# Local attention with stationary values in four column groups and weights normalised ahead of the transpose; causal mask added on VectorE; new instruction orders

## What is computed

```python
# block 1: attention, 16 heads of 64;  block 2: routed spline network (cheap, long chain of small steps)
# block 3, L1_attn
lin = linear_attention(h @ wq_lin, h @ wk_lin, h @ wv_lin)
# 16 heads of 8 channels, each query sees the keys at distance -32..32
s = q_loc . k_loc / sqrt(8) + rel_bias[offset, head];  a = softmax(s over the 65 offsets);  win = a @ v_loc
gate = sigmoid(relu([lin, win, h] @ wg1 + bg1) @ wg2 + bg2)
x = gate * lin + (1 - gate) * win, then @ wo + bo
# block 4, L1_ffn: sequences of 256, handled as the sub-sequences that the reference's shapes give
attn = softmax(causal(10 * l2norm(q) @ l2norm(k)));  16 heads of 64
moe = sum_e gate_e * (gelu(h @ w1_e + b1_e) @ w2_e + b2_e), 8 experts of 512
```

## Time and profile before

| | |
|---|---|
| runs | 2386.63, 2387.47, 2390.48 us (median 2387.47) |
| profiled execution, span from first to last instruction | 2377.5 us |
| PE (TensorE) busy | 2234.4 us, 94% |
| DVE (VectorE) busy | 1557.1 us, 65% |
| ACT (ScalarE) busy | 1348.7 us, 57% |
| POOL (GpSimd) busy | 847.3 us, 36% |
| chain that ended last | PE 77%, DVE 12%, ACT 5%, POOL 4% |
| mean granted TensorE clock | 0.986 |

### The profile page before, as it was taken

One profiled execution on the slowest core, in us unless ns is written; L12 is line 12 of the kernel. 1 busy time (PEld: TensorE's weight loads), 2 busy tenths in 40 slices (PEclk: granted clock), 3 DMA queues, 4 the chain that ended last, 5 costly groups with the idle time before them and its releaser, 6 DMA issues.

```text
span 2377.5 us, 44469 instructions
## 1 busy us (share of the span) xinstructions
PE 2234.4 (94%) x16347; PEld 1546.4 (65%) x16347; DVE 1557.1 (65%) x4247; ACT 1348.7 (57%) x3784; POOL 847.3 (36%) x1010
## 2 busy tenths in 40 slices
PE   8999999999999999999999999999999999999897
PEld 5565666856667566676667666676666756667465
DVE  5677676676657766577765867558675676656752
ACT  5346464764547755476545757466564764646452
POOL 3315551064510643116521356114561054510630
PEclk9999999999999999999999999999999999999999
DMA  4000001000010000110001000001001000010001
GB/s 149 28 1 1 1 2 45 10 32 1 1 54 11 23 1 1 54 33 1 1 10 45 32 1 1 27 28 32 1 1 45 10 32 1 1 36 10 32 1 49
DMA packets 24722, 50.46 MB, mean 21 GB/s; under 512 B 3316, under 2 KB 3900, under 8 KB 24252
## 3 DMA queue, kind: packets, MB, share of 16 engines
q1 hardware_dynamic: 24508, 47.63, 6.2%
HBM read 45.52 MB, written 2.10 MB: 20 GB/s over the span
## 4 chain that ended last, share of the span: by engine, by line
PE 77%; DVE 12%; ACT 5%; POOL 4%; issue 2%; DMA 0%; SPq 0%; DVEq 0%; ACTq 0%
PE ps L1494 10%; PE ps L1515 10%; PE ps L651 5%; PE ps L668 5%; PE ps L602 5%; PE ps L868 4%; PE ps L1428 4%; PE ps L906 4%; PE ps L1527 4%; PE ps L1445 4%; PE ps L799 3%; PE ps L782 3%; PE ps L835 2%; PE ps L1383 2%; PE ps L1394 2%; POOL rn L1737 2%
## 5 line engine op out<-in xcount | busy, mean ns | idle before, releaser
L1048 POOL TENSOR_TENSOR rstd<-ve,half_neg 128x4 f32<-128x4 f32 (+1 forms) x56 | 66.8, 1193 | 971.9 <-DVE ve L1029 971.9
L1515 PEld LDWEIGHTS ps<-wbuf,QK 128*128 128x128 f32 x2048 | 266.0, 191 | 108.2 <-issue 99.9
L1304 POOL TENSOR_TENSOR E<-E,ri 128x512 f32<-128x512 f32 x240 | 247.4, 1039 | 180.4 <-DVE ri L1103 180.2
L1618 ACT ACTIVATE QK<-ps,cols 128x512 f32<-128x512 f32 x256 | 172.7, 687 | 209.1 <-PE ps L1494 208.8
L1494 PE MATMUL ps<-h2T,wbuf 128*128 128x512 f32 x512 | 275.4, 626 | 0.2
L1744 POOL TENSOR_TENSOR work<-work,ri 128x128 f32<-128x128 f32 x480 | 231.2, 506 | 120.5 <-DVE ri L1667 119.7
L1515 PE MATMUL ps<-wbuf,QK 128*128 128x128 f32 x2048 | 270.2, 275 | 0.0
L929 ACT ACTIVATE E<-ps,nm 128x256 f32<-128x256 f32 x480 | 225.6, 485 | 64.3 <-DVE nm L1096 64.0
L1578 ACT ACTIVATE work<-ps,nm 128x128 f32<-128x128 f32 x480 | 198.5, 425 | 98.5 <-DVE nm L1658 98.4
L1737 POOL TENSOR_TENSOR rn<-ss,half_neg 128x8 f32<-128x8 f32 x120 | 195.1, 1637 | 156.8 <-DVE ss L1643 155.9
L1096 DVE TENSOR_REDUCE nm<-ps 128x2 f32<-128x512 f32 x256 | 168.8, 684 | 23.4 <-PE ps L651 21.7
(11 more groups left out here) (280 smaller groups left out, 4529.5 us busy)
## 6 DMA issues: line engine op xcount, KB each, us to landing
wbuf<-in_w SPq DMA_DIRECT2D x128, 256.0 KB, 3.2
xT<-in_xT SPq DMA_DIRECT2D x8, 256.0 KB, 3.5
xr<-in_xr SPq DMA_DIRECT2D x8, 256.0 KB, 4.2
bias_t<-in_bias_t SPq DMA_DIRECT2D x1, 2048.0 KB
out_y<-xn SPq DMA_DIRECT2D x8, 256.0 KB, 2.2
wqkv<-in_wqkv SPq DMA_DIRECT2D x1, 1536.0 KB
wo<-in_wo SPq DMA_DIRECT2D x2, 512.0 KB, 7.6
rows<-in_rows SPq DMA_DIRECT2D x1, 531.0 KB, 6.7
```

The source lines that it names most:

```text
L1304: nc.gpsimd.tensor_tensor(L.E[:, g % 4, :, :], L.E[:, g % 4, :, :], L.ri[:, g, :].unsqueeze(2).broadcast_to((P, NT, S)), ALU.mult)\
L1515: last = nc.tensor.matmul(bank2[2 + x % 2][:, t * P:(t + 1) * P], hid[:, x % 2, c, t * P:(t + 1) * P], w2[:, x % WB, c, :], start=(c == 0) ...
```

## The change

- **Values.** `VW` loses the column of ones. For four units of 128 queries x 4 heads each (n = 0 to 3, one half-sequence) `window_values` does 8 matmuls: 32 value channels (4 heads) are stationary, 256 weights move, and head group g goes to column group 32g of the array and of PSUM. Each output holds 4 queries-by-head blocks of which one is of use to a row.
- **Picking.** `picked_values` on VectorE multiplies by a 0/1 mask `only`, sums over the 4 blocks and, on every second n, adds the bias. The result lies in `winT` already transposed; `scaled`, `window_T` and `win_biased` go.
- **Normalising.** The exponentials keep a running sum (`accum_out`), VectorE takes its reciprocal (`inverse_sum`, once for each unit), GpSimd multiplies `Sw` (once for each unit), and only then TensorE transposes. `ETw` gets a twin, `ETx`. The transposes of units 2v-4 and 2v-3 come at step v, where they were units 2v-2 and 2v-1.
- **Causal mask.** L1420 goes. VectorE adds the mask to the scores in PSUM and takes the minimum of the negated sum in one `tensor_tensor_reduce` for each head and tile: 4 for each u, where 2 reductions were. The exponentials use scale -1, and those of a head wait for that head alone.
- **Set-up.** One memset less, one small VectorE step more, a wait for the GpSimd set-up before the first normalisation.
- **Orders.** All strings are new.

```diff
+            def window_values(n):
+                b, p = divmod(n, 2)
+                pe.wait_ge(s["w_et"], upto("w_et", 4 * n + 4))
+                if n:
+                    pe.wait_ge(s["w_picked"], upto("w_picked", n))
+                for j in range(2):
+                    for g in range(4):
+                        last = nc.tensor.matmul(bank1[3][32 * g:32 * (g + 1), j * S:(j + 1) * S],
+                                                VW[:, b, 2 * p + j, 32 * g:32 * (g + 1)],
+                                                ETq[n % 2][:, 4 * g + j:4 * g + 4:2, :],
+                                                start=True, stop=True, skip_group_check=True)
+                last.then_inc(s["w_av"], 1)
...
-                pe.wait_ge(s["w_exp"], upto("w_exp", V + 1))
+                pe.wait_ge(s["w_norm"], upto("w_norm", V + 1))
...
-                    for i in range(2):
-                        nc.tensor.matmul(tri(L.bank[i][:, 0:384], 3)[:, 0::2, :], ident_bf[:, :],
-                                         causal[:, :].unsqueeze(1).broadcast_to((P, 2, P)),
-                                         start=True, stop=False, skip_group_check=True)
...
-                                               bias=nmw[:, V % 4, hd:hd + 1])
+                                               bias=nmw[:, V % 4, hd:hd + 1], accum_out=rsw[:, V % 4, hd:hd + 1])
...
-            for v in range(4 * NP + 1):
+            for v in range(4 * NP + 2):
                 for i in range(2):
                     yield
-                    if v:
-                        window_copy(2 * v - 2 + i)
+                    if v >= 2:
+                        window_copy(2 * v - 4 + i)
...
+            def inverse_sum(V):
+                dve.wait_ge(s["w_exp"], upto("w_exp", V + 1))
+                nc.vector.reciprocal(riw[:, V % 4, :], rsw[:, V % 4, :]).then_inc(s["w_ri"], 1)
+            def picked_values(n):
+                b, p = divmod(n, 2)
+                dve.wait_ge(s["w_av"], upto("w_av", n + 1))
+                if n:
+                    dve.wait_ge(s["w_summed"], upto("w_summed", n))
+                nc.vector.tensor_tensor(picks[:, :, :, :], bank1[3].rearrange("p (t h q) -> p t h q", t=2, h=4),
+                                        only[:, :].unsqueeze(1).unsqueeze(3).broadcast_to((P, 2, 4, QT)), ALU.mult)\
+                    .then_inc(s["w_picked"], 1)
+                dve.wait_ge(s["w_picked"], upto("w_picked", n + 1))
+                nc.vector.tensor_reduce(tri(winT[:, b * S + p * P:b * S + (p + 1) * P], 2),
+                                        picks[:, :, :, :].rearrange("p t h q -> p t q h"), AX, ALU.add)\
+                    .then_inc(s["w_summed"], 1)
+                if p:
+                    dve.wait_ge(s["w_summed"], upto("w_summed", n + 1))
+                    nc.vector.tensor_scalar(winT[:, b * S:(b + 1) * S], winT[:, b * S:(b + 1) * S], col("bv_loc"), None,
+                                            ALU.add).then_inc(s["winT_ready"], 1)
...
+            for V in range(8 * NP):
+                yield
+                pool.wait_ge(s["w_ri"], upto("w_ri", V + 1))
+                nc.gpsimd.tensor_tensor(Sw[:, V % 4, :, :], Sw[:, V % 4, :, :],
+                                        riw[:, V % 4, :].unsqueeze(2).broadcast_to((P, 4, P)), ALU.mult)\
+                    .then_inc(s["w_norm"], 1)
...
-                    first_bank = 4 if L.bank is bank2 else 0
-                    for t in range(NT):
-                        ins = nc.vector.tensor_reduce(L.nm[:, 2 * u:2 * u + 2, t],
-                                                      ps[:, first_bank:first_bank + 2, t * P:t * P + (t + 1) * P],
-                                                      AX, ALU.max, negate=True)
-                    ins.then_inc(sem_of(L, "max"), 1)
+                    for i in range(2):
+                        for t in range(NT):
+                            o = L.bank[i][:, t * P:t * P + (t + 1) * P]
+                            ins = nc.vector.tensor_tensor_reduce(o, o, causal[:, (1 - t) * P:2 * P], -1.0, 3e38, ALU.add,
+                                                                 ALU.min, L.nm[:, 2 * u + i, t:t + 1])
+                        ins.then_inc(sem_of(L, "max"), 1)
```

More of the change, by code:

```diff
@@ new lines @@
+    ("both", "tensor"):
+        "000110111111101001110011011011101101111010110101010100101101011101010110101101010110010101100101"
+        "101101101011110101111101111001110111011011110101110101001010101100101011001101010010110010101101"
+        "001011010011010101010011010101101001101010111111111111101111111110111100101100101010110000000000"
+        "000000011000020020200202200222222",
+    ("last", "tensor"):
+        "001000001001010110110011001101011101011101101110101011001010101010101010100101010101100101011010"
+        "010110100101101001110010101011001001010000000000000000000000000000000000000000",
@@ L97 @@
[L97 to L101 removed]
+        "1101111111",
 }
@@ L127, in whole_net @@
         ident_bf = sb("ident_bf", [P, P], BF16)
-        causal = sb("causal", [P, P], BF16)
+        causal = sb("causal", [P, 2 * P])
         W0 = sb("W0", [P, 2, NH * DH])
@@ L228, in whole_net @@
         hidg, gt = qloc, kloc
-        VW = sb("VW", [P, NP, 4, WH, WD + 1])
+        VW = sb("VW", [P, NP, 4, D])
+        ETx = sb("ETx", [P, WH, P])
+        ETq = [ETw, ETx]
+        only = sb("only", [P, 4])
         nmw = sb("nmw", [P, 4, 4])
-        rsw = sb("rsw", [P, NP, 8 * 4])
-        win = sb("win", [P, NT, D])
+        rsw = sb("rsw", [P, 4, 4])
+        riw = sb("riw", [P, 4, 4])
         xh = sb("xh", [P, TT, D])
@@ L357, in setup_pool_consts @@
         def setup_pool_consts(pool):
[L358 to L359 removed]
+            for n, (ap, value) in enumerate(((half_neg[:, :], -0.5), (vlin1[:, :, D], 1.0), (gel[COMP:COMP + 1, :], 1.0),
+                                             (causal[:, :], 0.0))):
                 nc.gpsimd.memset(ap, value).then_inc(setup_pool, 1)
                 pool.wait_ge(setup_pool, n + 1)
[L362 removed]
+            nc.gpsimd.affine_select(out=causal[:, P:2 * P], in_=causal[:, P:2 * P], compare_op=ALU.is_ge, fill=CAUSAL_FILL,
                                     base=0, pattern=[[-1, P]], channel_multiplier=1).then_inc(setup_pool, 1)
@@ L385, in setup_cols @@
             link(dve, nc.vector.tensor_reduce(rowmask[:, :], col("headmask", 0, WH).rearrange("p (g j) -> p j g", j=4), AX, ALU.add))
+            link(dve, nc.vector.tensor_scalar(only[:, :], rowmask[:, :], 0.0, None, ALU.is_gt))
             sig = router[:, CL:CL + TILES]
-            raw = win[:, :, :].rearrange("p t n -> p (t n)")
+            raw = fT
             q, low = raw[:, 0:TILES], raw[:, TILES:2 * TILES]
@@ L783, in window_weights_T @@
                 last.then_inc(s["w_tr"], 1)
+            def window_values(n):
[10 more added lines that the diff above has]
+                last.then_inc(s["w_av"], 1)
             WU = 8 * NP
-            for v in range(WU // 2 + 2):
+            for v in range(WU // 2 + 3):
                 yield
@@ L885, in spare_work @@
                                  start=True, stop=True)
-        def window_T(b):
-            nc.tensor.wait_ge(s["w_scaled"], upto("w_scaled", b + 1))
-            for t in range(NT):
-                last = nc.tensor.transpose(bank1[3][:, t * P:(t + 1) * P], win[:, t, :], ident[:, :])
-            last.then_inc(s["win_tr"], 1)
         def et_wait(eng, L, n, g):
@@ new lines, in first_dve @@
+            for v in range(4 * NP + 3):
+                if v < 4 * NP:
+                    for i in range(2):
+                        yield
+                        V = 2 * v + i
+                        p, g = V // 4 % 2, V % 4
+                        dve.wait_ge(s["w_sc"], upto("w_sc", V + 1))
+                        if V >= 4:
+                            dve.wait_ge(s["w_tr"], upto("w_tr", V - 3))
+                        nc.vector.tensor_tensor(Sw[:, V % 4, :, :], tri(bank1[i], 4), bias_t[:, p, 4 * g:4 * g + 4, :],
+                                                ALU.add).then_inc(s["w_add"], 1)
+                        dve.wait_ge(s["w_add"], upto("w_add", V + 1))
+                        nc.vector.tensor_reduce(nmw[:, V % 4, :], Sw[:, V % 4, :, :], AX, ALU.max, negate=True)\
+                            .then_inc(s["w_max"], 1)
```

186 lines of the change are left out of this document (63 added, 123 removed).

## The result

The changed kernel takes **2482.1 us** (median of 2479.1 to 2484.4) where the kernel before takes 2389.0: a ratio of 1.040, interval 1.037 to 1.042. Slower, as forecast, but by 93 us and not by 15, and outside the range given. The profiled execution spans 2478.2 us for 2377.5, 100.7 more. Both numbers hold: every run here takes 1.8 us more than its span (2479.97 for 2478.2), so the profiled execution of the kernel before was one of some 2379 us, about 10 quicker than the median, and the 10 us between span and runs are no fixed part of a run.

What follows compares the result with a forecast made beforehand. TensorE was taken to bound both attention stages. First part +8.6, seven both parts (+4.4 - 3.0) x 7 = +9.8, last part -2.5: together +16 us on the 2377.5 us span, runs 10 above: 2403 us, range 2356 to 2440.

Steps and rivals of the forecast that it cites:

- Direction and bound: Whole kernel: slower, +16 us on the span; local attention leaves TensorE's bound for waits, attention stays bound by TensorE.
- The clock rival: Local attention: granted clock halves, up to +4 us in each of eight stages, +30 on the forecast, 2433 us; chance 0.08.
- a turn: Local attention: one round of two units, forecast to alternate between 4.65 and 5.3 us.
- The ring itself: Local attention: additions wait for transposes, these for GpSimd, GpSimd for reciprocals behind additions; 4.65 us for two units, 5.3 alternately.
- TensorE idles about 1.7 us in a turn: Local attention: TensorE's slack while the ring sets the pace, with the blocks between the same as before.
- Blocks in the ring: Local attention, both parts: feed-forward fill-in blocks unchanged, TensorE full up to the seventh add; gate +4.4 us later.
- blocks M: Local attention: fill-in blocks on TensorE, forecast to be the same before and after the change.
- The running sum: Local attention, exponentials: sum reads hidden under the ring, costing nothing; else 64 reads of 0.1 = 6 us a pair.
- Values: right.: Local attention, TensorE: 16 passes of 256 columns take 1.1 us with four column groups side by side, 2.1 otherwise.
- The mask on TensorE: Causal attention: without L1420 a head pair gives back 0.22 us, 3.5 us a both part.
- On VectorE: Causal attention: mask operations add 0.3 us a head pair (0 to 0.7), 5 us a part, covered by VectorE's slack.
- Right for the wrong reason: Causal attention: gains 3.0 us of a possible 3.5 in a both part, as VectorE stays at 71 to 78%.

Runs made afterwards that it cites:

- filled kernel: Changed kernel with unread matmuls put into TensorE's waits (filled waits) in local attention of the both parts: 2436.9 us, ratio 1.020.
- the filling: The unread matmuls in TensorE's waits; for the first part, the filled kernel with the same work there too: 2426.8 us, ratio 1.018.
- eight slots: Changed kernel with eight slots for the weights instead of four in both parts: 2446.6 us, ratio 1.024.
- a run on the filled kernel: Filled kernel with the last three gelus of the feed-forward computed as exponentials in both parts, removing two table loads: 2424.6 us, ratio 1.016.
- mask-only kernel: Kernel before with only the causal mask moved to VectorE, old orders and local attention kept: 2355.3 us, ratio 0.987.
- the late start: Mask-only kernel with the first head's exponentials waiting for the maxima of both heads, as before the change: 2379.9 us, ratio 0.999.
- the kernel with the early start: Kernel before, mask still on TensorE, with maxima taken head by head and the first head's exponentials waiting only for their own: 2382.5 us, ratio 0.999.

## Why the prediction was wrong, step by step

- **Direction and bound: right.** Local attention leaves TensorE's bound and turns into a ring of waits, and that costs more than the mask gives. The wait named is there: 130.0 us in 82 waits of the additions for L790, the longest 4.9.

```profile
DVE E L1254 <- PE ps L790: 130.0, 82, 4.9
```

- **The clock rival, given 0.08: it happened, and was too cheap.** "Local attention has no gap over 2 us" was the argument against; the clock fell all the same, in a stretch where TensorE was busy 7.26 of 10.1 us, much like the earlier trace rows (5.81 of 8.1), the row that I had read and weighed too lightly. The argument itself held, but for one wait of 2.2 us in the first part (in both parts none is over 1.4), and did not help. It was priced at 0.7 us a turn. Measured are 5.94 for 4.83 and 7.80 for 5.40: 1.1 and 2.4. The filled kernel puts it at 45 us in the seven both parts (6.4 us each); in the first part the filling made the stage 7 us shorter.
- **The ring itself: right at full clock, but one ring of two.** 5.3 and 4.65 us a turn were forecast, 5.40 and 4.83 to 5.09 measured with filled waits, and for the reasons given: in the turn from 1346.47 the values start at 1350.10, 3.6 us into it as forecast, behind ScalarE's copy, and push the transposes to 1351.10; in the next one the transposes at 1355.94 wait for GpSimd. The step that failed is "TensorE idles about 1.7 us in a turn": this slack was read as cover. It isn't free, because scores wait for the second addition and stand ahead of values and transposes. That second ring, 3.9 us (4.9 with values) at full clock, hid under the one I had; at half clock its pieces take 1.90 for 1.29, 1.19 for 0.70, 2.01 for 1.09 us and values 1.86 for 1.0, and then it is the bound. With eight slots, where the additions don't wait, the stage takes 57.7 us for 62.
- **Blocks in the ring.** That TensorE "does the same blocks M" and is full up to the seventh add failed for the first turns. For the both part at 1343.6, against the forecast of 51.4 us from the first scores (1287.6 before) to the second gate (1339.0):

| | forecast | changed | filled waits |
|---|---|---|---|
| first scores to seventh add | 19.3 | 22.9 | 23.6 |
| to the fifteenth add | 19.9 | 26.3 | 20.7 |
| to the second gate | 12.2 | 15.7 | 13.7 |

 The sums are 51.4, 64.9 and 58.0 us: of the 13.5 that I missed in such a part, 6.9 go with the clock and 6.6 are there without it. Of the 3.6 us in the first line, 1.3 are a table load, shown by a run on the filled kernel; that feed-forward blocks and the 16 reads make the rest is read from the trace, not shown. In the last line VectorE's accumulation waits for feed-forward blocks ahead of two reciprocals, and the picking reduction takes 1.05 us for the 0.73 that I took. The running sum, put at nothing, costs 1.7 us a part.
- **Values: right.** 1.07 us (forecast 1.1; 2.1 if two groups ran at a time). The Trainium skill, TensorE: Matmul & The Clock Gate, section "Packing small matmuls — row/col tiling", led to an estimate of 1.4; the trace decides for 1.07.
- **The mask on TensorE: not measured by itself.** 3.5 us a part were forecast. The 3.6 of the mask-only kernel are a net of less work on TensorE, a longer step on VectorE and an earlier first exponential, so that they agree is luck; with the late start nothing is left of them. **On VectorE: mis-sized**, +1.03 us a head pair for +0.3, and outside the bounds 0 to 0.7. I took the price from a two-input operation over 128 elements in a row of four (0.28); this one takes 0.31 and 0.47, and each has a read of 0.14 behind it. The rule of the Trainium skill, VectorE: DVE Perf Modes, section "Two Vector instructions with no wait between them", that an accumulator output makes a second instruction, agrees with the 512 reads in the trace; I had named it and set it aside, and had used a read of 0.1.
- **Right for the wrong reason:** attention gained, yet not because VectorE has slack. It gained because the earlier first exponential paid for the longer VectorE step (2379.9 without it, 2355.3 with it), a part of the change that I had mentioned but not priced. Attention's other 3.7 us a part are about 2 us of feed-forward steps that went into local attention, and about 1.5 us from the new orders.

## What to carry to other kernels

Before a stage is made to wait instead of to work, list every wait of the busiest engine's queue in one turn, not only the one that the edit adds, and compute the turn at both clock levels: a ring that hides under another at full clock can be the bound at half. Slack on TensorE isn't cover by itself; where a stage must wait, work without use put exactly into the waits (never between two steps of the chain) can pay, here 45 us of the 93. When an operation moves to another engine and gets longer there, see whether its first result can start its reader early: the move was worth 33 us with that and nothing measurable without.

## What the runs showed of the hardware, not expected

- Granted clock fell to half in a stage where no wait of TensorE was over 2.2 us (1.4 in both parts); with about 1.5 us of filling in a turn (busy 22.4 of 25.05 us) it stayed at 1.00.
- VectorE's add-and-minimum with an accumulator: 314 ns over 128 and 466 ns over 256 elements from PSUM, with 142 ns for the read. A plain reduction takes 286 and 415 ns (the kernel with the early start).
- VectorE's reduction of 512 elements to 128 over a strided innermost axis of 4 takes 1.05 us; that of 512 to 4 over adjacent elements 0.69.
- Four column groups side by side: 16 passes of 256 columns in fp32 in 1.07 us at full and 1.94 at half clock, where L668 with two groups has 0.135 us a pass, 2.2 for 16.
